# Depthwise convolution at the end of a four-layer kernel: four tap products on ScalarE, added in pairs on GpSimd, four taps on VectorE

## What is computed

```
def _L3_conv_ref(x, kernel):
    mask = jnp.ones((n, n, 1), dtype=kernel.dtype).at[n // 2, n // 2, 0].set(0.0)
    k = kernel * mask
    out = jax.lax.conv_general_dilated(x, k[:, :, None, :], window_strides=(1, 1),
              padding='SAME', dimension_numbers=('NHWC', 'HWIO', 'NHWC'), feature_group_count=ch)
    return out + x
```

## Time and profile before

| what | us |
|---|---|
| median of 3 runs (5062.12 to 5074.29) | 5062.19 |
| the profiled execution's own time | 5065.89 |
| its span | 5064.2 |
| the convolution's first load is issued, in the span | 4884.28 |
| its last tile is copied out | 5059.65 to 5060.67 |

### The profile page before, as it was taken

How to read it: one execution, slowest core, us unless ns; L and a number is a source line. 1 busy time by engine, 2 the same in 40 slices (tenths; PEclk the granted TensorE clock), 3 DMA queues, 4 the chain that set the end, 5 groups by cost and what they waited for, 6 DMA issues and landing times. The chain is left out here.

```text
span 5064.2 us, 210976 instructions
## 1 busy us (share of the span) xinstructions
PE 4728.5 (93%) x87632; PEld 4058.7 (80%) x87632; DVE 3492.4 (69%) x5701; ACT 2552.9 (50%) x6424; POOL 2224.7 (44%) x1165
## 2 busy tenths in 40 slices
PE   8999989999968999999789999998899989899967
PEld 6788867888845999999569999997788867788866
DVE  3788854888834666666546666664688864888866
ACT  5666646666613333333223333334667646676633
POOL 0699951999933000000320000000599960899930
PEclk9999999999978999999899999999999999999988
DMA  3000021000021000000110000002000012000012
GB/s 90 19 23 24 24 61 47 22 24 24 23 66 61 13 16 16 16 16 13 65 48 16 16 16 13 15 13 79 27 23 23 24 45 63 23 24 24 23 56 87
DMA packets 190089, 166.72 MB, mean 33 GB/s; under 512 B 26576, under 2 KB 184784, under 8 KB 189904
## 3 DMA queue, kind: packets, MB, share of 16 engines
q1 hardware_dynamic: 189904, 164.14, 10.8%
HBM read 113.74 MB, written 50.33 MB: 32 GB/s over the span
## 5 line engine op out<-in xcount | busy, mean ns | idle before, releaser
L860 POOL TENSOR_TENSOR tri_work<-tri_v,tri_work 128x1024 f32<-128x1024 f32 x768 | 1801.3, 2375 | 159.8 <-PE tri_psum L605 159.3
L779 DVE TENSOR_TENSOR tri_work<-tri_v,tri_psum 128x1024 f32<-128x1024 f32 x1280 | 1507.4, 1218 | 214.7 <-PE tri_psum L605 195.1
L605 PE MATMUL tri_psum<-tri_work 128*32 128x64 f32 x65536 | 1106.4, 221 | 36.9 <-issue 15.0
L605 PEld LDWEIGHTS tri_psum<-tri_work 128*32 128x32 f32 x65536 | 966.5, 110 | 192.0 <-issue 101.4
L1295 ACT ACTIVATE global_work<-global_psum 128x512 f32<-128x512 f32 x512 | 305.6, 597 | 1013.2 <-PE global_psum L1256 1013.2
L1370 POOL TENSOR_TENSOR global_work<-global_work,global_bp 128x256 f32<-128x256 f32 x64 | 46.7, 749 | 1576.1 <-DVE global_work L1327 1568.7
L1333 DVE TENSOR_REDUCE global_work<-global_work 128x1 f32<-128x512 f32 x512 | 348.9, 682 | 470.2 <-ACT global_work L1295 470.2
L1276 PE MATMUL global_psum<-global_v_high,global_pT_high 128*128 128x256 f32 x2048 | 610.8, 298 | 3.5 <-DVE global_pT_low L1351 3.5
L1276 PE MATMUL global_psum<-global_v_high,global_pT_low 128*128 128x256 f32 x2048 | 577.8, 282 | 0.0
L1276 PE MATMUL global_psum<-global_v_low,global_pT_high 128*128 128x256 f32 x2048 | 577.3, 282 | 0.0
L1256 PE MATMUL global_psum<-global_k_high,global_q_high 128*128 128x512 f32 x1024 | 422.0, 412 | 24.4 <-DVE global_q_low L1313 21.6
(11 more groups left out here) (140 smaller groups left out, 7831.2 us busy)
## 6 DMA issues: line engine op xcount, KB each, us to landing
tri_work<-in_x SPq DMA_DIRECT2D x192, 128.0 KB, 2.1
tri_work<-x SPq DMA_DIRECT2D x192, 128.0 KB, 2.0
x<-tri_work SPq DMA_DIRECT2D x128, 128.0 KB, 1.7
tri_work<-in_x SPq DMA_DIRECT2D x128, 64.0 KB, 2.2
global_work<-x SPq DMA_DIRECT2D x16, 512.0 KB, 4.2
xn<-global_work SPq DMA_DIRECT2D x16, 512.0 KB, 3.0
qT<-global_work SPq DMA_DIRECT2D x32, 256.0 KB, 2.1
global_work<-qT SPq DMA_DIRECT2D x64, 128.0 KB, 2.2
```

The lines of the kernel that those rows point to most:

```text
L605: mm = nc.tensor.matmul(psum[32 * g:32 * g + 32, OW, region * N:region * N + N], v1_diag[:, c * 32:c * 32 + 32], src[:, at_ * N:at_ * N + ...
L779: nc.vector.tensor_tensor(prod_d[k % 2].rearrange("p (d j) -> p d j", d=CU), v2[:, c:c + CU, :], psum[:, A[n.slot], (c // D) * N:(c // D + ...
L860: nc.gpsimd.tensor_tensor(prod_p[k % 2].rearrange("p (d j) -> p d j", d=CU), v2[:, c:c + CU, :], a_sb[n.slot][:, h * N:(h + 1) * N].unsque ...
```

## The change

ACT makes the products of four taps instead of two, in a buffer twice as large. POOL, which was idle here, adds them in pairs, in place: product 0 becomes 0 + 1, product 2 becomes 2 + 3, each as one instruction of 128 x 1024 (both halves). DVE keeps four taps, eight instructions a step instead of twelve. PE transposes back products 0 and 2 and the sum, as many instructions as before, and waits for the new semaphore `paired` in place of `products`.

```diff
-        prod = [sb(f"prod{k}", [P, 2, KC, BANK]) for k in range(2)]
+        prod = [sb(f"prod{k}", [P, 4, KC, BANK]) for k in range(2)]
...
-        PROD = TAPS[-2:]
-        SUMS = TAPS[:-2]
-        NS, NPR = len(SUMS) * KC, len(PROD) * KC
+        PROD = TAPS[-4:]
+        SUMS = TAPS[:-4]
+        NS, NPR, NPAIR = len(SUMS) * KC, len(PROD) * KC, 2
...
-                            pe.wait_ge(s["products"], after(g, NPR))
+                            pe.wait_ge(s["paired"], after(g, NPAIR))
                             pe.wait_ge(s["summed"], after(g, NS))
...
-                                    for q in range(len(PROD)):
+                                    for q in (0, 2):
...
+                @block.gpsimd
+                def _(pool):
+                    def body(g, i, ahead, now):
+                        if now:
+                            for a in range(NPAIR):
+                                pool.wait_ge(s["products"], after(g, NPR, (a + 1) * NPR // NPAIR))
+                                nc.gpsimd.tensor_tensor(prod[g.slot][:, 2 * a], prod[g.slot][:, 2 * a], prod[g.slot][:, 2 * a + 1],
+                                                        ALU.add).then_inc(s["paired"], 1)
+                    steps(pool, body)
```

More of the change, by code:

```diff
@@ L1392, in conv_layer @@
         acc = [sb(f"acc{k}", [P, KC, BANK]) for k in range(2)]
-        prod = [sb(f"prod{k}", [P, 2, KC, BANK]) for k in range(2)]
+        prod = [sb(f"prod{k}", [P, 4, KC, BANK]) for k in range(2)]
         tile = [sb(f"tile{k}", [P, 4, E]) for k in range(2)]
         img = image[:, :, :].rearrange("p k (r c) -> p k r c", c=NP)
-        names = ("taps_in", "cleared", "x_in0", "x_in1", "xT_mm", "image_copy", "summed", "products", "back_mm", "back_copy", "out0", "out1", "sp_settled")
+        names = ("taps_in", "cleared", "x_in0", "x_in1", "xT_mm", "image_copy", "summed", "products", "paired", "back_mm", "back_copy", "out0", "out1", "sp_settled")
         s = {k: sem(k) for k in names}
```

## The result

The changed kernel took 5094.8 us (median of 4 runs, 5089.06 to 5095.65), the kernel before 5064.7 us (median of 4): the ratio is 1.005, with a 95% interval of 1.0038 to 1.0062. Timed again in five rounds it took 5083.54 us against 5062.26, ratio 1.0037 (1.0024 to 1.0051). It is slower, by 21 to 30 us; 20 were forecast. The profiled execution took 5094.96 us, with a span of 5093.0.

The account below looks back on a forecast made before the run. The prediction took a ring of waits in the convolution, not DVE's own work, as the bound. Middle gaps +7.4, first gaps +6.8 and last pairs +6.0 gave +20 us: 5082.4 us, 8-in-10 range 5061 to 5118.

Parts of the forecast that it names:

- the ring: Convolution: sum, back step, transposes and image copy wait on each other in turn, 17.92 us, against DVE's own 15.92.
- the gaps: Convolution: time from the first sum of one pair of steps to that of the next, 17.48 to 18.86 us before.
- Turns between DVE and POOL: Convolution: DVE's sums and POOL's adds exclude each other, 0.13 us hidden per change; a step takes 9.46 us, not 7.96.
- Who gets in: Convolution sums: a waiting POOL add was assumed to get in at the next boundary between two DVE instructions.
- The rival in which DVE keeps its turn: Convolution: the sum runs through (5.30 us), adds follow between sums; +56 us, 5118 us; chance 0.18.
- First gaps: From first to second pair of steps in each image: 21.97 us, +3.4 each, +6.8 for two.
- Middle gaps: Second and third of each image, four in all: 19.9 us, +1.85 each, +7.4 together.
- Last pairs: Last two steps of each image, to the last copy-out's end: 25.88 us, +3.0 each, +6.0 for two.
- The back step: PE's transposing back in each convolution step, ahead of the next transposes: taken as 7.56 us, range 7.09 to 8.03.
- The total: Whole kernel: 5062.2 + 20.2 = 5082.4 us, 0.4% slower; the forecast's own range 5077 to 5095.
- The second rival: Convolution: sums do not exclude adds, which end as late as the sum did; no slower, 5062 us; chance 0.20.

Follow-up runs that it names:

- another kernel: The changed kernel with PE transposing the rows of step g+3 instead of g+2 ahead of the back step of g: 5079.13 us, one run.

## Why the prediction was right

- **The bound.** That the ring sum, back step, transposes, image copy sets the gaps was right: with the rows turned earlier the gaps of the kernel before fell from 18.0 to 15.9 us, DVE's own work.
- **Turns between DVE and POOL.** Right, and shown by one edit: with the second input in PSUM nothing is held. A step's sum and adds took 9.53 us (9.46 predicted); an add that comes out of a wait took 2.20 us (2.21) and a DVE instruction 0.56 (0.53). That the place of the inputs decides is shown for two-input instructions only: the cast in the earlier trace rows was held too, with one input, and no run here tests why.
- **Who gets in.** In the changed kernel every add got in at the next boundary between DVE's instructions, as assumed: none lasted over 2981 ns. The rival in which DVE keeps its turn did not come true there, though four adds of another kernel show that it can happen. That an add gets in at once was an assumption, as the prediction says, and no row stood behind it.
- **The terms.** First gaps: 21.97 predicted, 22.31 and 21.13 measured. Middle gaps: 19.9 predicted, 20.51, 20.21, 19.90 and 19.21 measured, mean 19.96. Last pairs: 25.88 predicted, 25.83 and 25.84 measured. The convolution's +19.9 us stands against +20.2. Two of the four middle gaps lie outside the 19.5 to 20.4 that I gave.
- **The back step.** Its mean was right, in part by luck, for its reason did not hold. I took 7.56 us because PE would wait longer ahead of it; in the six gaps it took 6.80 to 8.10, mean 7.59. But the wait ahead does not set it: 4.96 us of waiting stand ahead of the one of 8.10, and 8.81 ahead of the one of 6.80 (5015.13 to 5021.93), where the granted clock was 0.79:

```profile
5015.13 1.23 PE L1482 MATMUL conv_psum<-eye,conv_prod 128*128 128x128 f32 x4 [8.81 <-DVE conv_acc L1545]
```

```profile
5015.13:5021.93 6.80, 6.80 (x48) 6.80 (x49) 6.80 (x8) 0.00 (x0) 2.15 (x1) 0.79 0.00 0
```

- **The total.** The first comparison gave +30 us, inside the range but 10 above the forecast; its 5094.8 us lie just under the 5095 that the forecast's own range ends at. The term at fault is not in the sum: I held the layers ahead to be equal in both, and they differ by up to 16 us between executions. In the second profile of the changed kernel they took 5 us less than in the kernel before (4873.32 against 4878.75). The second comparison gave +21.
- **The second rival,** in which sums and adds don't exclude each other, gave 5062 us for itself. The kernel with the sum in PSUM, which takes the exclusion away almost wholly, took 5068.7 against 5067.4: the rival's own arithmetic, that the adds end as late as the sum did, was right, and its premise wrong.
- **The rule of the Trainium skill** (SBUF — State Buffer, "SBUF: two separate sides") agrees: two SBUF inputs against a GpSimd read. The measured turns are a little shorter than whole durations: an add by 0.14 us (2.20 against 2.34) and a DVE instruction by 0.10 (0.56 against the 0.663 from one start to the next), where the prediction hid 0.13 of each.

## What to carry to other kernels

Work moved from VectorE to GpSimd is not beside it when VectorE's instructions have two SBUF inputs and GpSimd's read SBUF: here each pair add took 2.1 us of the sum's time and freed 1.3. Look for the inputs' place before the durations, and keep a running sum in PSUM where banks allow. And find the ring first: the shorter sum in PSUM gave nothing by itself (ratio 1.0003). Moving the transposes gave 0.998 by itself, and both together 0.9961.

## What the runs showed of the hardware that was not expected

Where both wait, DVE and POOL alternate one instruction each in the changed kernel, and an add hides 0.14 us of its start in its wait, a DVE instruction 0.10; but four adds in one kernel waited for a row of up to five DVE instructions. The back step, the same work each time, took 5.4 us at a granted clock of 1.00, 6.8 at 0.79 and 8.1 at 0.66. PE had waited 0.85, 8.81 and 4.96 us ahead of them, so the length of that one wait does not order them.
